# Two transformer blocks on one core: relative products shared by a pair of images, loads image by image, steps re-placed

## The chip, the cores and the metric

The kernel runs on one core of one Trainium2 chip. Its engines work from their own instruction queues and meet only through semaphores: TensorE (PE in the profile, with its weight loads as PEld), VectorE (DVE), ScalarE (ACT), GpSimd (POOL) and SyncE (SP, here the only one that issues DMAs). The metric is the device time of one execution in microseconds, as the median of several.

## The reference

The input is x, 8 images of 16x16 tokens with 192 channels, in float32. It goes through two blocks of the same form, each with its own weights, one after the other:

```
xn = layer_norm(x)                             # eps 1e-5 in block 0, 1e-6 in block 1
windows of 14x14 of xn padded to 28x28         # four windows an image, three of them mostly padding
q, k, v = xn @ qkv_w + qkv_b                   # 12 heads of 16 channels
attn = q*0.25 @ k.T                            # within a window
attn += rel_h[..., :, None] + rel_w[..., None, :]
#   rel_h = einsum("bhwc,hkc->bhwk", q, rel_pos_h[coords]), rel_w alike, along the other axis
out = softmax(attn) @ v
x = x + out @ proj_w + proj_b
x = x + gelu(layer_norm(x) @ fc1_w + fc1_b) @ fc2_w + fc2_b    # 192 -> 768 -> 192, exact gelu
```

Everything is held in float32. Several products are made of high and low parts of a rounded type (F32R), so that they come near float32.

## The kernel before, in words

**Tiling.** An image is 256 tokens, two tiles of 128. X stays in SBUF for all 8 images and both blocks, so there are 16 passes "n" (image n % 8 of block L = n // 8); `par` is n % 2 and chooses one of two buffers. The windows need no padding in memory: a mask row in the stacks keeps tokens of other windows apart, and small steps named pad_* add what the padded keys give to a softmax.

**A pass.** Its steps, in order:

- front: stats1, root1, hat1 normalise; PE transposes (`norm1`, L837, L839); ACT and DVE split the result in high and low parts (L521, L522, L677, L678); the q, k and v products (L831) go one after the other through the one PSUM bank FB, each evacuated by DVE.
- relative products (`front`, L903 to L919): for each of the two axes (w = 0, 1) 14 matmuls, one stationary matrix `rel_heads` (96x84) for each row or column i of the window. Rows 14 and 15 of the image use the matrices of rows 0 and 1, so for i = 0, 1 the moving operand is two rows (64 columns), else one (32 columns). A float32 matmul is two records in the trace. ACT evacuates w = 0 (L555), DVE w = 1 (L715); `rel_tok` (L920) brings what the pads need to token order.
- stacks: ACT, POOL split q, k and rel in high and low parts; SP copies them by DMA (L308, L329) into q_stack and k_stack, together with constant rows for the positions and the mask; one buffer of each for even and one for odd passes, in two groups of 6 heads.
- by_query (L971): scores with queries on partitions, for the row maxima alone (DVE, L768). top and neg_top; SP puts the negated maxima into the stack.
- by_key (L940): scores again with keys on partitions, ACT exponentiates (L530); times_v (L957) multiplies by v_ones, v with a column of ones.
- back: to_tokens (L1053), att, proj (L1040), x_att, stats2, root2, hat2, norm2 (L837 once more), low2, fc1 (L976), gelu (L595), fc2 (L1073), x_mlp.

**Order.** Each engine's program is unrolled by `run` from a table of its own (PE_AT, ACT_AT, DVE_AT, POOL_AT, SP_AT). A table gives each step a tick; step s of pass n is issued at tick 48 n + AT[s], and an engine issues its steps in the order of ticks. Ticks are an order and no times, and they are not comparable from one engine to another. In this way TensorE mixes by_query of pass n, the front of pass n+1, by_key of n-1 and the back of n-2.

**Start.** SP loads image 0, constants and block 0's qkv weights, copies the constant rows into both stacks by DMA (L289), loads the 7 other images at once (L293), then the proj and fc2 weights of both blocks (L294 to L301) on one semaphore `s_w`, then fc1's weights. POOL rounds the constant rows first (L389).

Of the kernel before, what the change touches and what calls it, by code (L numbers as in the profile page):

```python
# [5 lines left out]
F32 = mybir.dt.float32  # L6
F32R = mybir.dt.float32r
ALU = mybir.AluOpType
# [3 lines left out]
P = 128  # L12
# [3 lines left out]
HEADS = 12  # L16
# [11 lines left out]
NV = 3  # L28
# [10 lines left out]
ZEROED = 7 + 2 * NV  # L39
# [3 lines left out]
W_LOADS = 16 * 2 * 5  # L43
# [20 lines left out]
SP_AT = dict(qk0=-10, rel0=2, stack1=37, neg_top=66, wqkv=7, w1=-19, out=213)  # L64
# [5 lines left out]
def build(nc, x, layers, const, out):  # L70
# [3 lines left out]
    with ExitStack() as ctx:  # L74
# [43 lines left out]
        xhat = [sb(f"xhat{i}", [P, TILES, D]) for i in range(2)]  # L118
        xn_hi = [sb(f"xn_hi{i}", [P, 2, TOK], F32R) for i in range(2)]
        rows_rounded = xn_hi[1]  # L120
        xn_lo = [sb(f"xn_lo{i}", [P, TOK], F32R) for i in range(2)]
        q_t = sb("q_t", [GF, 2, TOK])
        k_t = sb("k_t", [GF, 2, TOK])
        q_grid = sb("q_grid", [GF, 2, TOK])
# [4 lines left out]
        rel_t = sb("rel_t", [GR, 2, 2, TOK])  # L129
# [25 lines left out]
        for L in range(2):  # L155
            rel.append(att[0:GF, L, 0:2 * (2 * WS - 1)].rearrange("p (w o) -> p w o", w=2))
# [990 lines left out]
```

## Time and profile before

| | us |
|---|---|
| median of 3 runs | 670.36 (660.64 to 671.58) |
| profiled execution, own time | 666.7 |
| its span, first to last instruction | 664.8 |
| PE busy / PEld busy | 558.1 (84%) / 502.5 (76%) |
| DVE / ACT / POOL busy | 361.0 (54%) / 305.5 (46%) / 236.1 (36%) |
| relative products, L917 | 87.7 busy, 896 records |
| by_query, L971 / row maxima, L768 | 84.8 / 130.7 |
| by_key, L940 / exps, L530 | 89.7 / 103.5 |
| fc2, L1073 | 70.9 |

Matmuls are pipelined, so busy times of neighbours overlap and a group's mean is longer than its pace. PEclk is the clock that TensorE was granted, as a share of its 2.4 GHz; it has two levels, 1.0 and 0.5. A wait names who released the waiting instruction last. The page's slices show PE idle in the third and fourth fortieth of the span and busy at 0.8 to 0.9 from then on.

### The profile page before, as it was taken

How to read it: one execution, taken by the hardware profiler on the slowest of the kernel's cores; microseconds unless marked ns; L12 is line 12 of the kernel's file. 1: busy time of each engine (PE TensorE's matmuls, PEld its weight loads, DVE VectorE, ACT ScalarE, POOL GpSimd, SP SyncE). 2: the span in 40 equal slices, each digit the busy share in tenths (PEclk: the TensorE clock that was granted, in tenths of full speed). 3: DMA queues.
4: the chain of work that ended last, by engine and by line, in shares of the span. 5: the costliest groups of instructions: out<-in, count | busy, mean ns of one | idle time of the engine just before them, and what ended most of it. 6: DMA issues, size and time to landing. Idle time of an engine off the chain costs nothing.

```text
span 664.8 us, 12602 instructions
## 1 busy us (share of the span) xinstructions
PE 558.1 (84%) x4440; PEld 502.5 (76%) x4440; DVE 361.0 (54%) x914; ACT 305.5 (46%) x614; POOL 236.1 (36%) x424
## 2 busy tenths in 40 slices
PE   5700778989898989899998989898989998978766
PEld 4700667779797979798897978797979887967646
DVE  3210265685848484856448575758584767473221
ACT  1100113347463736464344737474745574746522
POOL 2001354253625343441515252354444263430100
PEclk9999977599989898997689988999897999999777
DMA  4416523322222222224112222222231323220000
GB/s 99 107 47 172 107 52 70 85 68 69 52 54 58 58 59 58 59 58 101 42 37 45 61 55 58 59 57 61 57 72 43 86 53 76 57 71 27 1 12 13
DMA packets 45674, 41.10 MB, mean 62 GB/s; under 512 B 6268, under 2 KB 44588, under 8 KB 45612
## 3 DMA queue, kind: packets, MB, share of 16 engines
q1 hardware_dynamic: 45612, 40.29, 25.9%
q8 instruction: 36, 0.59, 0.4%
q14 instruction: 26, 0.21, 0.1%
HBM read 6.80 MB, written 1.57 MB: 13 GB/s over the span
## 4 chain that ended last, share of the span: by engine, by line
PE 55%; issue 13%; DVE 9%; SPq 9%; POOL 8%; ACT 3%; DMA 3%; POOLq 0%; DVEq 0%; ACTq 0%
PE front L917 11%; PE back L831 10%; PE back L1073 9%; PE by_key L940 5%; PE by_query L971 5%; PE front L831 4%; DVE xhat L671 3%; SPq L297 3%; PE times_v L957 2%; POOL norm_rstd L394 2%; SPq L293 2%; POOL pad_e L423 2%; SPq L289 2%; PE back L1053 1%; DVE att L750 1%
## 5 line engine op out<-in xcount | busy, mean ns | idle before, releaser
L768 DVE TENSOR_REDUCE row_max<-by_query 128x2 f32<-128x512 f32 x192 | 130.7, 682 | 48.9 <-PE by_query L971 47.7
L530 ACT ACTIVATE probs<-by_key 128x452 f32<-128x452 f32 x192 | 103.5, 543 | 84.9 <-PE by_key L940 84.3
L940 PE MATMUL by_key<-q_stack,k_stack 110*128 110x196 f32 (+1 forms) x384 | 89.7, 331 | 2.2 <-ACT probs L530 1.9
L971 PE MATMUL by_query<-k_stack,q_stack 108*128 108x256 f32 x384 | 84.8, 314 | 8.0 <-DMA q_stack<-rel_lo 7.7
L917 PEld LDWEIGHTS front<-q_grid,rel_heads 96*84 96x84 f32 x896 | 86.9, 181 | 3.8 <-ACT rel_t L556 1.9
L917 PE MATMUL front<-q_grid,rel_heads 96*84 96x32 f32 (+1 forms) x896 | 87.7, 265 | 2.2 <-ACT rel_t L556 1.4
L940 PEld LDWEIGHTS by_key<-q_stack,k_stack 110*128 110x128 f32 x384 | 63.9, 210 | 14.7 <-issue 7.3
L971 PEld LDWEIGHTS by_query<-k_stack,q_stack 108*128 108x128 f32 x384 | 65.5, 213 | 10.0 <-DMA q_stack<-rel_lo 9.5
L1073 PE MATMUL back<-w,hid 128*128 128x192 f32 x384 | 70.9, 337 | 0.4 <-ACT hid L595 0.3
L1073 PEld LDWEIGHTS back<-w,hid 128*128 128x128 f32 x384 | 65.0, 198 | 1.2 <-ACT hid L595 0.8
L831 PE MATMUL back<-xn_hi,w_hi 128*128 128x256 f32 x192 | 61.3, 328 | 2.7 <-DVE xn_hi L678 2.7
L831 PE MATMUL back<-xn_hi,w_lo 128*128 128x256 f32 x192 | 60.3, 323 | 0.0
L394 POOL TENSOR_TENSOR norm_rstd<-norm_var,minus_half 128x2 f32<-128x2 f32 x32 | 30.0, 939 | 75.4 <-DVE norm_var L663 74.1
L671 DVE TENSOR_TENSOR xhat<-xhat,norm_rstd 128x384 f32<-128x384 f32 x32 | 32.0, 1001 | 42.9 <-POOL norm_rstd L394 42.9
L715 DVE COPY rel_t<-front 84x448 f32<-84x448 f32 x16 | 9.9, 621 | 82.0 <-PE front L917 82.0
L448 POOL TENSOR_TENSOR pad_w<-pad_w,pad_prod 128x36 f32<-128x36 f32 x16 | 4.2, 263 | 138.5 <-ACT pad_w L570 138.5
L831 PEld LDWEIGHTS back<-xn_hi,w_hi 128*128 128x128 f32 x192 | 45.7, 238 | 3.6 <-DVE xn_hi L678 3.6
L957 PE MATMUL times_v<-probs,v_ones 128*32 128x256 f32 (+1 forms) x768 | 48.2, 370 | 0.0
L831 PEld LDWEIGHTS back<-xn_hi,w_lo 128*128 128x128 f32 x192 | 45.2, 236 | 0.0
L488 POOL CAST rel_hi<-rel_t 84x512 fp32r<-84x512 f32 x32 | 19.5, 609 | 71.9 <-DVE rel_t L716 59.0
L595 ACT ACTIVATE hid<-back,b_real 128x256 f32<-128x256 f32 x96 | 38.8, 473 | 10.6 <-PE back L831 10.4
L490 POOL TENSOR_TENSOR rel_lo<-rel_t,rel_hi 84x512 fp32r<-84x512 f32 x32 | 40.8, 1276 | 2.6
(142 smaller groups left out, 1102.7 us busy)
## 6 DMA issues: line engine op xcount, KB each, us to landing
q_stack<-q_hi SPq DMA_DIRECT2D x64, 96.0 KB
k_stack<-k_hi SPq DMA_DIRECT2D x64, 96.0 KB
q_stack<-rel_hi SPq DMA_DIRECT2D x64, 84.0 KB
q_stack<-rel_lo SPq DMA_DIRECT2D x64, 84.0 KB
q_stack<-q_lo SPq DMA_DIRECT2D x32, 96.0 KB
k_stack<-k_lo SPq DMA_DIRECT2D x32, 96.0 KB
out<-X SPq DMA_DIRECT2D x8, 192.0 KB, 2.2
k_stack<-xn_hi SPq DMA_DIRECT2D x2, 744.0 KB
```

Source lines behind the costliest of these rows:

```text
L394: pool.tensor_tensor(norm_rstd[i][:, :], norm_var[i][:, :], minus_half[:, :], ALU.pow).then_inc(n_rstd[i], 1)
L490: pool.tensor_tensor(rel_lo[par][:, w, :, :], rel_t[:, w, :, :], rel_hi[par][:, w, :, :].bitcast(F32), ALU.subtract).then_inc(s_rlo, 1)
L530: act.activation(probs[h % NP][:, :], KB[h % 2][:, 0:KEYS], ACT.Exp).then_inc(s_ex, 1)
L595: act.activation(hid[:, m, :], fc1_psum(m), ACT.Gelu, bias=b1_real[L][:, m:m + 1]).then_inc(s_ge, 1)
L671: dve.tensor_tensor(xhat[i][:, :, :], xhat[i][:, :, :], norm_rstd[i][:, :].unsqueeze(2).broadcast_to([P, TILES, D]), ALU.mult).then_inc(n_ ...
L768: dve.tensor_reduce(row_max[:, h, :], QB[h % 2][:, :].rearrange("p (a t) -> p a t", a=TILES), AX, ALU.max).then_inc(s_smax, 1)
L831: last = pe.matmul(psum, lhs, rhs, start=(i == 0), stop=(i == len(chunks) - 1))
L917: last = pe.matmul(dst[:, :, at, :], rel_heads[L][:, w, WS - 1 - i:2 * WS - 1 - i, :] .rearrange("p k h -> p (k h)"), grid[:, :, at, :], s ...
L940: last = pe.matmul(KB[h % 2][:, lo:hi], k_stack[par][0:ROWS, h, c * P:(c + 1) * P], q_stack[par][0:ROWS, h, 0:hi - lo], start=True, stop=True)
L957: last = pe.matmul(VB[i * VW:(i + 1) * VW, 0:hi - lo], v_ones[n % NV][:, c, h, :], probs[h % NP][:, lo:hi], start=(c == 1), stop=(c == 0))
L971: last = pe.matmul(QB[h % 2][:, a * TOK:(a + 1) * TOK], q_stack[par][0:R_MAX, h, a * P:(a + 1) * P], k_stack[par][0:R_MAX, h, :], start=Tr ...
L1073: last = pe.matmul(BB[0][:, a * D:(a + 1) * D], hid[:, m, a * P:(a + 1) * P], w2[L][:, m, :], start=(m == 0), stop=(m == MC - 1))
```

## The change

1. Relative products are made for a pair of images (n even, n+1). q_grid and rel_t hold both. Each axis is two blocks ("halves") of 8 matmuls; one matmul takes one row (or column) of both images, 64 columns, with one stationary matrix. The steps rel0 and rel1 become `rel` with four places in PE_AT; ACT evacuates two blocks, DVE two. q_t and k_t are double-buffered.
2. The 7 other images are loaded one by one, each with its semaphore. proj_b, fc2_b and the back weights have semaphores of their own by block, and are loaded at `late`. fc1's weights of block 0 come ahead of the first stack loads. The stack constants are written by ACT straight into the stacks (`stack_constants`), not rounded by POOL and copied by DMA. The fc1 bias product goes from pass 1 to pass 2 of a block.
3. Memory: v_ones has 17 columns a head for 32 and 5 buffers for 3; the rest of VB is zeroed once by a DVE memset. pad_e lies in rel_tok, and xhat of norm2 in att, with a wait for each (`s_psum` in rel_tok, `n_tr[1]` in att).
4. All places in the five tables are new. Many steps of the front have a place for even and one for odd passes. SP takes neg_top(n) ahead of stack1(n+1), and all eight stores behind everything else. The three gelu steps stand behind the 12 exps.

The diff, cut:

```diff
-NV = 3
+NV = 5
-ZEROED = 7 + 2 * NV
+ZEROED = 7 + NV
-W_LOADS = 16 * 2 * 5
+W_LOADS = 16 * 3
...
-PE_AT = dict(bias0=-42, bias1=-51, bias2=-48, norm1=-47, q=-41, k=-35, v=-30, rel0=-21, rel1=-15, rel_tok=-11,
-             by_query=(5, 6, 10, 14, 18, 22, 25, 29, 31, 34, 39, 42), neg_top=52,
-             by_key=(56, 60, 62, 65, 72, 76, 77, 81, 83, 87, 92, 96), times_v=(74, 87, 104), to_tokens=106, att=110,
-             proj=114, norm2=123, fc1=(127, 128, 132), fc2=(140, 148))
-ACT_AT = dict(weights1=-45, weights2=40, norm1=-46, q_hi=-35, q_grid=-36, k_hi=-27, rel0=-14, rel_tok=-1, pad_e=26, pad_w=63,
-              att=116, neg_top=51, probs=(62, 64, 68, 74, 76, 78, 82, 86, 90, 95, 99, 103), norm2=124,
-              gelu=(132, 135, 137))
-DVE_AT = dict(stats1=-58, hat1=-52, low1=-47, weights1=-45, weights2=47, bias0=-43, bias1=-50, bias2=-49, setup=-31, q=-42, k=-32, v=-23,
-              rel1=-17, pad_max=15, pad_sum=27, pad_top=34,
-              row_max=(5, 9, 13, 15, 19, 25, 27, 28, 32, 37, 40, 43), top=45, times_v=(78, 88, 105), att=108,
-              x_att=116, stats2=120, hat2=120, low2=123, x_mlp=149)
-POOL_AT = dict(norm_b=-45, root1=-46, proj_bias=-32, pad_shift=23, pad_join=30, pad_arg=59, pad_mul=59, pad_sum=66,
-               pad_out=78, fc2_bias=128, root2=121, q_lo=-21, k_lo=-22, rel0=-6, rel1=-4)
-SP_AT = dict(qk0=-10, rel0=2, stack1=37, neg_top=66, wqkv=7, w1=-19, out=213)
+PE_AT = dict(bias0=-64, bias1=-70, bias2=-74, norm1=(-68, -75), q=(-63, -68), k=(-52, -65), v=(-48, -61),
+             rel=(-5, -2, 0, 7), rel_tok=(17, 7), by_query=(41, 42, 48, 50, 51, 59, 60, 67, 70, 71, 74, 75),
+             neg_top=78, by_key=(84, 86, 91, 92, 94, 95, 101, 102, 103, 106, 109, 111), times_v=(101, 115, 123),
+             to_tokens=131, att=141, proj=144, norm2=157, fc1=(165, 169, 173), fc2=(173, 175))
+ACT_AT = dict(constants=(-83, 0), weights1=-80, weights2=98, norm1=(-54, -58), q_hi=-7, q_grid=(2, -46), k_hi=0,
+              rel=(7, 15), rel_tok=(31, 31), pad_e=58, pad_w=110, att=154, neg_top=94,
+              probs=(99, 101, 103, 105, 109, 111, 114, 118, 119, 121, 128, 129), norm2=169, gelu=(178, 183, 186))
+DVE_AT = dict(stats1=(-111, -114), hat1=(-92, -101), low1=(-67, -73), weights1=-84, weights2=82, bias0=-66,
+              bias1=-71, bias2=-87, setup=-46, q=(-59, -68), k=(-53, -68), v=(-52, -61), rel=(-4, 3), pad_max=28,
+              pad_sum=43, pad_top=58, row_max=(37, 42, 43, 44, 45, 53, 55, 56, 64, 67, 73, 74), top=75,
+              times_v=(100, 110, 126), att=133, x_att=139, stats2=141, hat2=141, low2=150, x_mlp=176)
+POOL_AT = dict(norm_b=-110, root1=(-158, -157), proj_bias=(-118, 19), pad_shift=-22, pad_join=-4, pad_arg=29,
+               pad_mul=42, pad_sum=42, pad_out=71, fc2_bias=104, root2=102, q_lo=-59, k_lo=-59, rel0=(-37, -91),
+               rel1=(-35, -75))
+SP_AT = dict(x=-878, late=-274, qk0=-350, rel0=-347, stack1=-328, neg_top=-283, wqkv=-254, w1=-356, out=1733)
...
-            for par in range(2):
-                sp.wait_ge(s_rounded, 1)
-                for stack, lo, hi, c in ((q_stack, R_MASK, R_MAX, 1), (k_stack, R_RHI, ROWS, 0)):
-                    sp.dma_start(stack[par][lo:hi, :, :].bitcast(F32),
-                                 rows_rounded[lo:hi, c:c + 1, :].bitcast(F32).broadcast_to([hi - lo, HEADS, TOK])
-                                 ).then_inc(s_stack0[par], 16)
-                if par == 0:
-                    sp.dma_start(X[:, TILES:, :], x_t[:, TILES:, :]).then_inc(s_x, 16)
-            for L in range(2):
+
+            def load_late(L):
                 p = layers[L]
-                for tile, name in ((pb[L], "proj_b"), (b2[L], "fc2_b")):
-                    sp.dma_start(tile[:, :], p[name].unsqueeze(0).broadcast_to([P, D])).then_inc(s_w, 16)
+                if L == 1:
+                    sp.dma_start(pb[1][:, :], p["proj_b"].unsqueeze(0).broadcast_to([P, D])).then_inc(s_pb[1], 16)
+                sp.dma_start(b2[L][:, :], p["fc2_b"].unsqueeze(0).broadcast_to([P, D])).then_inc(s_b2[L], 16)
                 sp.wait_ge(s_wz, L + 1)
-                sp.dma_start(wp[L][:, 0, :], p["proj_w"][0:P, :]).then_inc(s_w, 16)
-                sp.dma_start(wp[L][0:LO, 1, :], p["proj_w"][P:D, :]).then_inc(s_w, 16)
-                sp.dma_start(w2[L][:, :, :], p["fc2_w"].rearrange("(m f) n -> f m n", f=P)).then_inc(s_w, 16)
-            sp.wait_ge(s_wxl, 1)
-            sp.wait_ge(s_wxh, 2)
-            sp.wait_ge(s_bx, 1)
-            load_w1(0)
+                sp.dma_start(wp[L][:, 0, :], p["proj_w"][0:P, :]).then_inc(s_w[L], 16)
+                sp.dma_start(wp[L][0:LO, 1, :], p["proj_w"][P:D, :]).then_inc(s_w[L], 16)
+                sp.dma_start(w2[L][:, :, :], p["fc2_w"].rearrange("(m f) n -> f m n", f=P)).then_inc(s_w[L], 16)
+
+            def setup(n, L, par, t):
+                if t == SP_AT["x"] and 1 <= n < IMAGES:
+                    sp.dma_start(x_slot(0, n), x_t[:, n * TILES:(n + 1) * TILES, :]).then_inc(s_x[n], 16)
+                if t == SP_AT["late"] and n in (0, 2):
+                    load_late(n // 2)
...
+                    if n < 2:
+                        sp.wait_ge(s_stack0, 2 * (n + 1))
...
+                    src = rel_t[:, w, 2 * par:2 * par + 2, :]
+                    pool.wait_ge(s_relo, 4 * (n // 2) + 2 * w + 2)
+                    for g in range(2):
+                        if n >= 2:
+                            pool.wait_ge(*stack_loaded(n - 2, g))
+                    pool.tensor_copy(rel_hi[par][:, w, :, :], src).then_inc(s_rhi[par], 1)
+                    pool.wait_ge(s_rhi[par], done)
+                    pool.tensor_tensor(rel_lo[par][:, w, :, :], src, rel_hi[par][:, w, :, :].bitcast(F32),
+                                       ALU.subtract).then_inc(s_rlo[par], 1)
...
+            def stack_constants(par):
+                act.wait_ge(s_rows, 32)
+                for stack, rows in ((k_stack, key_rows), (q_stack, query_rows)):
+                    act.activation(stack[par][:, :, :], rows.unsqueeze(1).broadcast_to([P, HEADS, TOK]),
+                                   ACT.Copy).then_inc(s_stack0, 1)
+
             def weights(n, L, par, t):
+                if t in ACT_AT["constants"] and n == 0:
+                    stack_constants(ACT_AT["constants"].index(t))
...
+                if t in ACT_AT["rel"] and par == 0:
+                    half = ACT_AT["rel"].index(t)
+                    act.wait_ge(s_rel, 2 * n + half + 1)
+                    if n > 0:
+                        act.wait_ge(s_rt, n)
+                        for i in range(2):
+                            act.wait_ge(s_rlo[i], n)
+                    rows = slice(half * 8, half * 8 + 8)
+                    out, src = rel_t[:, 0, :, :], FB[0:GR, :].rearrange("p (m r c) -> p m r c", m=4, c=SIDE)
+                    act.activation(tall(out)[:, :, rows, :], src[:, :, :, 0:WS], ACT.Copy)
+                    act.activation(edge(out)[:, :, rows, :], src[:, :, :, WS:SIDE], ACT.Copy).then_inc(s_relo, 1)
...
+                if t in DVE_AT["rel"] and par == 0:
+                    half = DVE_AT["rel"].index(t)
+                    dve.wait_ge(s_rel, 2 * n + 3 + half)
+                    if n > 0:
+                        dve.wait_ge(s_rt, n)
+                        for i in range(2):
+                            dve.wait_ge(s_rlo[i], n)
+                    out, src = rel_t[:, 1, :, :], FB[0:GR, :].rearrange("p (m c r) -> p m r c", m=4, r=SIDE)
+                    if half == 0:
+                        last = dve.tensor_copy(tall(out)[:, :, :, 0:8], src)
+                    else:
+                        dve.tensor_copy(tall(out)[:, :, :, 8:WS], src[:, :, :, 0:WS - 8])
+                        last = dve.tensor_copy(edge(out), src[:, :, :, WS - 8:8])
+                    last.then_inc(s_relo, 1)
...
-                    for i in range(WS):
-                        at = slice(i, i + WS + 1, WS) if i < EDGE else slice(i, i + 1)
-                        last = pe.matmul(dst[:, :, at, :], rel_heads[L][:, w, WS - 1 - i:2 * WS - 1 - i, :]
-                                         .rearrange("p k h -> p (k h)"), grid[:, :, at, :], start=True, stop=True)
+                        pe.wait_ge(s_relo, 2 * n + 2 * w + half)
+                    grid = q_grid[:, :, :].rearrange("p m (r c) -> p m r c" if w == 0 else "p m (r c) -> p m c r", c=SIDE)
+                    dst = FB[0:GR, :].rearrange("p (m r c) -> p m r c", m=4, c=SIDE)
+                    for j in range(8):
+                        i = (half * 8 + j) % WS
+                        last = pe.matmul(dst[:, :, j, :], rel_heads[L][:, w, WS - 1 - i:2 * WS - 1 - i, :]
+                                         .rearrange("p k h -> p (k h)"), grid[:, :, half * 8 + j, :], start=True, stop=True)
                     last.then_inc(s_rel, 1)
...
```

Other lines of the diff give the new semaphores, choose the `[par]` place of a step, and index q_t and k_t by par.

## Rows read from the trace of the kernel before

**Rows 1.** The page's first line.

```profile
span 664.8 us, 12602 instructions
```

**Rows 2.** Windows: start:end, length, busy time (instructions) by engine, TensorE clock, DMA share, GB/s.

```profile
519.30:582.00 62.70, 58.68 (x541) 53.12 (x541) 41.58 (x103) 37.16 (x74) 28.32 (x49) 1.00 0.28 68
...
582.00:664.80 82.80, 61.09 (x417) 51.25 (x415) 29.93 (x79) 35.52 (x64) 11.61 (x25) 0.83 0.09 25
...
129.20:519.30 390.10, 363.71 (x3038) 331.95 (x3037) 247.50 (x626) 211.55 (x427) 160.62 (x275) 0.90 0.26 59
...
77.60:129.20 51.60, 43.92 (x304) 39.01 (x305) 30.02 (x73) 14.34 (x35) 21.97 (x41) 0.73 0.33 71
```

**Rows 3.** Chain of waits at the start: start us, us, what.

```profile
5.06 2.76 DMA hid<-c_query_rows
...
10.15 14.94 SPq L293
...
34.31 15.12 SPq L297
...
74.45 3.15 DMA q_stack<-rel_lo
```

**Rows 4.** Waits of the run: who for whom, us in total, times, longest.

```profile
POOL X L399 <- DMA w<-in_fc_w: 55.2, 1, 55.2
...
PE front L844 <- DMA weights_in<-in_fc_w: 30.8, 1, 30.8
```

**Rows 5.** Waits from 129.2 to 582 us.

```profile
PE back L837 <- DVE xhat L671: 20.9, 13, 1.8
```

**Rows 6.** Timelines (start, length, engine, what, idle time before) and a window: a norm2 stop.

```profile
212.12 0.41 PE L837 MATMUL back<-ident,xhat 128*128 128x128 f32 x2 [1.76 <-DVE xhat L671]
...
212.00:219.00 7.00, 6.88 (x49) 6.89 (x50) 3.88 (x9) 3.39 (x7) 5.64 (x13) 0.63 0.13 33
...
5.45 0.56 DVE L671 TENSOR_TENSOR xhat<-xhat,norm_rstd 128x384 f32<-128x384 f32 x1 [0.60 <-POOL norm_rstd L394]
...
279.73 1.61 DVE L671 TENSOR_TENSOR xhat<-xhat,norm_rstd 128x384 f32<-128x384 f32 x1 [0.59 <-POOL norm_rstd L394]
```

**Rows 7.** Relative products: timelines of four 64-column records each, one block on the chain.

```profile
287.39 0.61 PE L917 MATMUL front<-q_grid,rel_heads 96*84 96x64 f32 x4
...
361.80 0.45 PE L917 MATMUL front<-q_grid,rel_heads 96*84 96x64 f32 x4
...
287.56 2.21 PE front L917 x28
```

**Rows 8.** Timeline of the start, image 0's front and the fc1 bias product.

```profile
6.15 0.66 PE L837 MATMUL front<-ident,xhat 128*128 128x128 f32 x2 [6.15 <-DVE xhat L671]
...
7.82 1.43 ACT L500 ACTIVATE wqkv_hi<-weights_in,columns 128x576 fp32r<-128x576 f32 x2
...
8.39 0.42 DVE L678 TENSOR_TENSOR xn_hi<-front,xn_hi 64x256 fp32r<-64x256 f32 x1
...
14.02 0.53 PE L831 MATMUL front<-xn_hi,wqkv_hi 128*96 128x256 f32 x1
...
24.00 4.13 PE L917 MATMUL front<-q_grid,rel_heads 96*84 96x64 f32 x28 [0.65 <-DVE v_ones L705]
...
28.87 4.13 PE L917 MATMUL front<-q_grid,rel_heads 96*84 96x64 f32 x28 [0.74 <-ACT rel_t L556]
...
66.15 0.58 PE L844 MATMUL front<-columns,weights_in 128*128 128x1 f32 x2 [30.76 <-DMA weights_in<-in_fc_w]
...
73.14 0.66 PE L837 MATMUL front<-ident,xhat 128*128 128x128 f32 x2 [0.77 <-DVE b_real L623]
```

**Rows 9.** Timeline of SyncE's queue: two kinds of stack loads.

```profile
69.84 0.60 SPq L308 DMA_DIRECT2D k_stack<-k_hi  x1
...
71.76 1.80 SPq L329 DMA_DIRECT2D q_stack<-rel_hi  x2
```

**Rows 10.** Groups by line: name, shapes, count, busy us, mean ns, idle before.

```profile
L595 ACT ACT_TABLE_LOAD x31 | 39.8, 1283 | 0.5
```

More of the change, by code:

```diff
@@ L117, in build @@
         norm_rstd = [sb(f"norm_rstd{i}", [P, TILES]) for i in range(2)]
-        xhat = [sb(f"xhat{i}", [P, TILES, D]) for i in range(2)]
         xn_hi = [sb(f"xn_hi{i}", [P, 2, TOK], F32R) for i in range(2)]
-        rows_rounded = xn_hi[1]
         xn_lo = [sb(f"xn_lo{i}", [P, TOK], F32R) for i in range(2)]
-        q_t = sb("q_t", [GF, 2, TOK])
-        k_t = sb("k_t", [GF, 2, TOK])
-        q_grid = sb("q_grid", [GF, 2, TOK])
+        q_t = [sb(f"q_t{i}", [GF, 2, TOK]) for i in range(2)]
+        k_t = [sb(f"k_t{i}", [GF, 2, TOK]) for i in range(2)]
+        q_grid = sb("q_grid", [GF, 4, TOK])
         q_hi = [sb(f"q_hi{i}", [GF, 2, TOK], F32R) for i in range(2)]
@@ L135, in build @@
         k_stack = [sb(f"k_stack{i}", [P, HEADS, TOK], F32R) for i in range(2)]
-        v_ones = [sb(f"v_ones{i}", [P, TILES, HEADS, VW]) for i in range(NV)]
-        pad_e = sb("pad_e", [P, 2 * HEADS, WS])
+        v_ones = [sb(f"v_ones{i}", [P, TILES, HEADS, HD + 1]) for i in range(NV)]
+        pad_e = rel_tok[:, 0:2 * HEADS * WS].rearrange("p (h k) -> p h k", k=WS)
         seg_max = [sb(f"seg_max{i}", [P, 2, HEADS]) for i in range(2)]
@@ L154, in build @@
         att = sb("att", [P, TILES, 2 * P])
+        xhat = [sb("xhat", [P, TILES, D]), att[:, :, 0:D]]
         for L in range(2):
@@ L210, in build @@
         s_rt, s_rto = sem("rel_transposed"), sem("rel_tok_ready")
-        s_rhi, s_rlo = sem("rel_hi"), sem("rel_lo")
+        s_rhi, s_rlo = ([sem(f"{x}{i}") for i in range(2)] for x in ("rel_hi", "rel_lo"))
         s_v = sem("v_ready")
@@ L517, in norm_hi @@
                 act.wait_ge(s_vp if i == 0 else s_f1, n if i == 0 else MC * n)
-                if i == 1 and n == 0:
-                    for par in range(2):
-                        act.wait_ge(s_stack0[par], 32)
                 act.activation(xn_hi[i][:, 0, :], bank[:, 0:TOK], ACT.Copy)
@@ L582, in norms @@
             def norms(n, L, par, t):
-                if t == ACT_AT["norm1"]:
+                if t == ACT_AT["norm1"][par]:
                     norm_hi(0, n, FB)
@@ L896, in front @@
                                           slice(at + g * GF, at + (g + 1) * GF))
-                    last.then_inc(s_qp if t == PE_AT["q"] else s_kp, 1)
-                if t == PE_AT["v"]:
+                    last.then_inc(s_qp if t == PE_AT["q"][par] else s_kp, 1)
+                if t == PE_AT["v"][par]:
                     pe.wait_ge(s_kto, n + 1)
@@ L902, in front, with rel_products @@
                     last.then_inc(s_vp, 1)
-                if t in (PE_AT["rel0"], PE_AT["rel1"]):
-                    w = (PE_AT["rel0"], PE_AT["rel1"]).index(t)
-                    if w == 0:
-                        pe.wait_ge(s_v, n + 1)
-                        pe.wait_ge(s_qg, n + 1)
+            def rel_products(n, L, par, t):
+                if t in PE_AT["rel"] and par == 0:
+                    w, half = divmod(PE_AT["rel"].index(t), 2)
+                    if w + half == 0:
+                        pe.wait_ge(s_v, n + 2)
+                        pe.wait_ge(s_qg, n + 2)
@@ L922, in front, with rel_tokens @@
+                    last.then_inc(s_rel, 1)
+            def rel_tokens(n, L, par, t):
+                if t == PE_AT["rel_tok"][par]:
+                    if par == 0:
+                        pe.wait_ge(s_relo, 2 * n + 4)
+                    elif n + 1 < 2 * IMAGES:
+                        pe.wait_ge(s_v, n + 2)
+                    else:
+                        pe.wait_ge(s_rto, n)
                     for w in range(2):
@@ L956, in times_v @@
                             h = g * QUAD + i
[L957 removed]
+                            last = pe.matmul(VB[i * VW:i * VW + HD + 1, 0:hi - lo], v_ones[n % NV][:, c, h, :],
                                              probs[h % NP][:, lo:hi], start=(c == 1), stop=(c == 0))
@@ L1075, in back @@
                     last.then_inc(s_f2, 1)
-            run(PE_AT, biases, stacks, middle, front, back, times_v, scores_by_key, to_tokens)
+            run(PE_AT, biases, stacks, middle, front, rel_products, rel_tokens, back, times_v, scores_by_key, to_tokens)
 def kernel(**inputs):
```

180 lines of the change are left out of this document (76 added, 104 removed).

## The prediction

> **What bounds the kernel now.** I read the page, the chain, the waits, then single stretches. The span is 664.8 us [rows 1]. Four stretches, cut at the first by_query product of images 0, 2, 13 and 15, show what each is worth [rows 2]. (a) Up to 77.65 us nothing of the scores runs. The reader is to see in the chain that SyncE's queue holds it [rows 3]: the 1344 KB load of X occupies it for 14.94 us, and after a copy of constants the first bias broadcast 15.12. GpSimd then waits 55.2 us for the last back weight, because `s_w` counts both layers, and TensorE 30.8 us for fc1's weights [rows 4]. (b) Images 0 to 2: 51.6 us for two periods. (c) 129.2 to 582.0: 13 periods. TensorE is busy 363.7 of 390.1 us, then 58.7 of 62.7; it is the bound. A period is 390.1/11 = 35.5 us at clock 0.90, but 62.7/2 = 31.4 us where the clock is 1.00. (d) The last 82.8 us, busy 61.1, clock 0.83.
>
> In (c) there is one repeated stop: the norm2 transposes wait 20.9 us in 13 times for xhat [rows 5]. In the stop at 212.12 it lasts 1.76 us, and the seven microseconds from 212 have a clock of 0.63 [rows 6]. In that chain VectorE's multiplication takes 1.61 us; at the start of the kernel, with GpSimd idle, the same took 0.56 [rows 6]. In steady state GpSimd works on k_lo beside it.
>
> **Relative products.** Before: per image 14 stationaries for each of two axes, two records each, 56 records. After: per pair 4 blocks of 8 matmuls, 64 records of 64 columns instead of 112 of mostly 32; over the run 512 for 896. A block of 28 takes 2.21 us on the chain at clock 1.00 [rows 7], 0.075 us a record allowing for its wider ones. Four 64-column records of the column axis, which reads with a stride of 16 elements, cover 0.61 us where four of the row axis cover 0.45 [rows 7]: 0.16 more, of which I give 0.05 to the last one's own length, so about 0.11 us a record against 0.075. Before, a pair is 56 x 0.075 + 48 x 0.075 + 8 x 0.11 = 8.7 us; after, 32 x 0.075 + 32 x 0.11 = 5.9. That is 2.8 a pair, 1.4 an image, all on the bound. Bounds: 0.075 for all (3.9 a pair) and 0.61/4 = 0.15 for the strided (1.5 a pair): 9 us less and 10 more over the run.
>
> The Trainium skill, "TensorE: Matmul & The Clock Gate", Back-to-back issue gap, has every product of 1 to 64 columns cost the same, which would be the first of these bounds: 31 us saved in all where my rows say 22. The strided row is what speaks against it here.
>
> Between the four blocks one bank is evacuated: 0.74 us at the start (28.13 to 28.87) [rows 8]. In the steady order two by_key heads, and sometimes the att transposes, stand between rel.0 and rel.1, only two heads between rel.1 and rel.2, and much between rel.2 and rel.3. I charge 1 us a pair, 6.5 over 13 periods. The by_key and by_query heads now go in twos against two banks; 0.1 us of wait a period is 1.5. Together **+8**; bounds 0 and +20 (four uncovered evacuations of 0.74 in each of 6.5 pairs).
>
> **Start.** X goes as 192 KB loads, fc1's as soon as qkv's buffer is free, proj and fc2 weights after image 1's stacks. The pieces of X still need the queue, but image 1 needs only the first of them, and nothing else is wanted before some 36 us; cover gone, it costs up to 14.94 us. The stack constants come from ScalarE. Two qkv weight activations of 576 columns take 1.43 us [rows 8], so 3072 columns at about 0.9 ns each are 2.9 us, two per parity 5.8 (upper bound 7.6 at 1.24 ns). The rows' transfer took 2.76 [rows 3], is now second in the queue, lands near 4.5; the constants end at 10.3, weights at 11.8, norm_hi and the low part at 13.5. Before, q starts at 14.02, after the bias product [rows 8]; I take 14.5. q, k, v are 10 us (14.02 to 24.00): 24.5. Image 1 has to go through FB too before the first rel block: 2.7 us from transposes (6.15) to low part (8.81), plus 10: 37.2. ScalarE's second pair of constants, 5.8 us, fits beside that. Four blocks at the start's pace of 4.13 x 16/28 = 2.36, plus 0.74 each: 49.6. rel_tok, eight small records at that pace, and one evacuation: about 2.2 (an estimate), 51.8. The fc1 bias product, moved to image 2, is ahead of the first by_query: 7.0 us to the next transposes (66.15 to 73.14) [rows 8], then norm1(2) 2.7 and q(2) 2.3 (two thirds of a third of the 10 us above): **64**. The stack of image 0 lands before: GpSimd's two parts of the last axis (2 us, an estimate), SyncE's four issues at 0.9, landing 3.15 [rows 3, 9] make 58.4. So 77.65 becomes 64; bounds 58 (bias product at full clock) and 78 (no gain).
>
> **Norm2.** Between proj and norm2 the order now has four by_query and four or five by_key heads, one times_v group and rel_tok or rel.3: 42 records or more at 58.7/541 = 0.11 us [rows 2], 4.5 us. The chain from proj to xhat lost 1.76 us to a shorter cover with hat2 at 1.61; fc2_bias, which waits for hat2, and not k_lo now follows root2, so a microsecond of the chain goes as well. The stop goes: **-20.9** in (c). What is late next is hat2 itself in VectorE's queue, behind row maxima, covered by one more microsecond only. Bounds 0 and -25.
>
> **Clock.** At 0.90 over 390.1 us, 39.0 us are lost. Behind the stop of [rows 6] the clock fell, and the stretch without a fall is the one in which I take the stops to be shorter. Not every fall need have that cause, so I take two thirds back: **-26**, bounds 0 and -39. The same skill page, in the table of why this matters, warns only of long idle gaps between bursts, so by it stops this short would not lower the clock and this term would be nothing: that is rival A. That 519.3 to 582.0 stayed at 1.00 is for my view [rows 2].
>
> **Other edits at no cost.** Gelus stand in one group after the exps: table loads fall from 31 for gelu (and as many back) to 16, 1.28 us each [rows 10]. ScalarE is busy 37.2 of 62.7 us [rows 2], so it counts only in (d), where gelu and exp alternate on the chain: -3 there. New waits: att waits for norm2's transposes of the image before (xhat shares it), two microseconds or more ahead in the order; rel_tok waits for pad_sum, since pad_e shares it, with 36 of 48 ticks between; rel_hi and rel_lo wait for the stack of n-2, loaded a period earlier. q_t and k_t doubled only remove waits. v_ones at 17 columns, NV 5, a memset of VB: nothing. The eight stores are issued after the last neg_top; the first six are of finished images and go beside some 60 us of TensorE work. w1 and qkv reloads wait on SyncE for scaled halves as before.
>
> **Sum.** (a) 64; (b) 51.6 - 2.8 = 48.8; (c) 452.8 - 18.2 - 20.9 - 26 + 8 = 395.7; (d) 80: 588.5 us of span. The profiled execution took 666.7 for 664.8, so 590.4. It lay 3.7 us under the median of the three runs (670.36); put back, **594 us**.
>
> **Rivals.**
> A. The stops move rather than go, and the clock stays (for: another wait lies one microsecond behind; that every fall has its stop isn't shown; against: the 31.4 us periods). Then (c) is 452.8 - 18.2 + 8 = 442.6 and the median 641. Chance 0.15.
> B. The start gives nothing: two fronts, constants and the bias product take until 78 us. For: three tasks were put in front; against: 30 us of queueing in [rows 3] are gone. 608. Chance 0.08.
> C. Slower. SyncE takes neg_top(n) before the second half of stack n+1 and all of n+2. Place: by_query's seventh head of image n+1. After neg_top(n), six issues at 0.60 and four at 0.9 plus 3.15 of landing are 10.4 us [rows 3, 9]; TensorE's order up to that head holds about half of a period, 15 us. From 4.6 us of extra delay (the qk rows held by by_key of n-1, or k_lo late behind GpSimd's rel parts) each further microsecond costs 15. At 6.5 beyond it 98 are lost, more than the 76 gained: about 692. The queue's waits before, and by_query not among the long waits in (c), speak against. Chance 0.03.
> D. Strided products at 0.15 us or evacuations uncovered: the rel part saves almost nothing, 594 + 20 = 614. Chance 0.08.
> My forecast, 0.66: 570 to 615.
>
> **Range.** Down: all of the clock (-13), no new hand-offs (-8), bias product fast (-3) give 570. Up: D, B, and a part of A up to 638, where the clock returns by little. What is left out is most of A's upper half and C, about a tenth, and somewhat less below. A measurement of this kernel tells about 2% (13 us) from no change. Faster by more than that: A, B, D and the forecast, 0.94 with a margin for the unforeseen; within, 0.03; slower 0.03.
>
> **What would show it.** L917 with 512 records, the four-record test 0.45 and 0.61; first by_query near 64; no wait of back L837 over 1 us; table loads halved; periods near 30 us with clock over 0.95. By_query waiting for q_stack's transfer is C, L837 or another back wait of 1.5 us with the clock at 0.90 is A. It is wrong if periods stay at 33 us or more.

## The result and the profile after

The changed kernel takes 545.72 us (median of 4 runs, 545.31 to 546.63) where the kernel before took 668.19 beside it (660.64 to 671.58): ratio 0.82, 95% interval 0.8124 to 0.8275. Ratios are of fast executions alone; where the kernel before stands beside a run below, its time is the median of those of its executions that lie within 1.5% of the fastest. The forecast was 594, the range 570 to 638. The direction was right; the gain was 1.6 times the forecast one, 122 us instead of 76.

The page after: span, TensorE's busy tenths and the clock's.

```profile
span 543.9 us, 11882 instructions
...
PE   2777878889999999999999999999999999999947
...
PEclk9999998989999999999979999999999999999988
```

The profiled execution took 545.7 us for this span. TensorE is busy for 90% or more of each slice from the tenth to the thirty-eighth, and the clock's row has hardly a dent. Cut at the same places, first by_query of images 0, 2 and 15 (columns as in [rows 2]):

```profile
0.00:65.70 65.70, 43.15 (x198) 37.76 (x199) 19.64 (x58) 20.67 (x28) 19.19 (x41) 1.00 0.36 84
65.70:109.60 43.90, 36.55 (x284) 29.12 (x283) 32.02 (x76) 15.40 (x39) 23.76 (x43) 0.96 0.42 92
109.60:476.30 366.70, 362.23 (x3191) 328.57 (x3190) 275.27 (x701) 209.47 (x463) 177.88 (x316) 0.99 0.33 75
476.30:543.90 67.60, 53.11 (x389) 44.39 (x388) 27.27 (x75) 27.45 (x58) 10.91 (x24) 0.92 0.13 35
```

Stretch (c) as one window of the kernel before:

```profile
129.20:582.00 452.80, 422.38 (x3577) 385.07 (x3576) 289.07 (x729) 248.71 (x501) 188.94 (x324) 0.92 0.26 60
```

So (a) went from 77.6 to 65.7, (b) from 51.6 to 43.9, (c) from 452.8 to 366.7, (d) from 82.8 to 67.6. In (c) the norm2 stops of [rows 5] are gone. The longest wait of TensorE left there (columns as in [rows 4]); the only other one is 1.5 us in all:

```profile
PE front L844 <- DVE q_t L695: 2.4, 2, 1.6
```

VectorE's second multiplication, the 1.61 us of [rows 6], is short in steady state now (timeline). Relative records are 512, as forecast, and table loads for gelu 15, where the forecast had 16 (groups by line as in [rows 10]):

```profile
297.58 0.56 DVE L677 TENSOR_TENSOR att<-att,norm_rstd 128x384 f32<-128x384 f32 x1
```

```profile
L931 PE MATMUL front<-q_grid,rel_heads 96*84 96x64 f32 x512 | 56.4, 273 | 4.0 <-ACT rel_t L562 2.5
```

### The profile page after: what moved, and what is told of

Read it like the earlier page. It is cut to its first block, busy times and chain, and to the rows that moved or that the text cites. A ratio compares the mean times of both kernels' runs of the same rounds, so it can differ in the third digit from the quotient of the medians.

```text
span 543.9 us, 11882 instructions
## 1 busy us (share of the span) xinstructions
PE 495.0 (91%) x4056; PEld 439.8 (81%) x4056; DVE 354.2 (65%) x907; ACT 273.0 (50%) x586; POOL 231.7 (43%) x422
## 4 chain that ended last, share of the span: by engine, by line
PE 81%; issue 9%; DVE 6%; ACT 1%; DMA 1%; POOL 1%; SPq 1%; DVEq 0%; ACTq 0%; POOLq 0%
PE back L844 14%; PE front L844 12%; PE back L1094 10%; PE front L931 10%; PE by_key L961 9%; PE by_query L990 8%; PE times_v L978 7%; DVE row_max L782 1%; PE front L858 1%; PE front L949 1%; PE front L857 1%; PE front L850 1%; PE back L1074 1%; PE front L946 1%; PE back L850 1%
## 5 line engine op out<-in xcount | busy, mean ns | idle before, releaser
L961 PE MATMUL by_key<-q_stack,k_stack 110*128 110x196 f32 (+1 forms) x384 | 73.5, 308 | 1.5 <-ACT probs L532 1.2
L990 PE MATMUL by_query<-k_stack,q_stack 108*128 108x256 f32 x384 | 69.4, 295 | 1.4 <-DVE row_max L782 1.0
L414 POOL TENSOR_TENSOR rel_tok<-rel_tok,seg_max 128x48 f32<-128x48 f32 (+1 forms) x32 | 14.6, 479 | 115.4 <-DVE seg_max L739 115.4
L961 PEld LDWEIGHTS by_key<-q_stack,k_stack 110*128 110x128 f32 x384 | 53.6, 193 | 11.2 <-issue 5.5
L931 PE MATMUL front<-q_grid,rel_heads 96*84 96x64 f32 x512 | 56.4, 273 | 4.0 <-ACT rel_t L562 2.5
L931 PEld LDWEIGHTS front<-q_grid,rel_heads 96*84 96x84 f32 x512 | 53.0, 173 | 5.7 <-ACT rel_t L562 3.3
L844 PE MATMUL front<-xn_hi,wqkv_hi 128*96 128x256 f32 x128 | 40.7, 327 | 9.8 <-DVE q_t L695 4.9
L978 PE MATMUL times_v<-probs,v_ones 128*17 128x256 f32 (+1 forms) x768 | 47.5, 366 | 0.0
L844 PE MATMUL front<-xn_hi,wqkv_lo 128*96 128x256 f32 x128 | 38.0, 306 | 0.0
L844 PEld LDWEIGHTS front<-xn_hi,wqkv_hi 128*96 128x96 f32 x128 | 23.4, 183 | 15.4 <-DVE xn_hi L684 8.2
```

Source lines behind the costliest of these rows:

```text
L414: last = pool.tensor_tensor(pad_e[:, :, lo:hi], pad_e[:, :, lo:hi], m.broadcast_to([P, 2 * HEADS, hi - lo]), ALU.subtract)
L844: last = pe.matmul(psum, lhs, rhs, start=(i == 0), stop=(i == len(chunks) - 1))
L931: last = pe.matmul(dst[:, :, j, :], rel_heads[L][:, w, WS - 1 - i:2 * WS - 1 - i, :] .rearrange("p k h -> p (k h)"), grid[:, :, half * 8 + ...
L961: last = pe.matmul(KB[h % 2][:, lo:hi], k_stack[par][0:ROWS, h, c * P:(c + 1) * P], q_stack[par][0:ROWS, h, 0:hi - lo], start=True, stop=True)
L978: last = pe.matmul(VB[i * VW:i * VW + HD + 1, 0:hi - lo], v_ones[n % NV][:, c, h, :], probs[h % NP][:, lo:hi], start=(c == 1), stop=(c == 0))
L990: last = pe.matmul(QB[h % 2][:, a * TOK:(a + 1) * TOK], q_stack[par][0:R_MAX, h, a * P:(a + 1) * P], k_stack[par][0:R_MAX, h, :], start=Tr ...
```

## Experiments

Theory: a short stop of TensorE ahead of norm2 costs its own length and, behind it, clock; the clock gave back more than the forecast's 26 us. Rival: stop and clock are separate, and the surplus comes from fewer records or fewer table loads. Clock loss below is (1 - mean clock) x span of the profiled run; it is 65 us in the kernel before (0.902 x 664.8) and 12 in the changed one (0.978 x 543.9). It leaves out the start: the trace's record of the clock begins with the first change of level, at 80.6 us in the kernel before and at 68.1 in the changed one, and the rows' 1.00 ahead of that is no reading. The products show the level instead: 256 columns start 0.21 us apart until just before 68 us in the changed kernel and 0.12 apart behind it, and the kernel before goes from one distance to the other at 80.6 us.

### Edits of the kernel before

These four ran beside a kernel before of 656.1 us (four runs, 652.27 to 660.28; all seven reach to 678.25). Its mean clock in these four was 0.914 to 0.927, a clock loss of about 51 us.

**Stop filled.** Ahead of the norm2 transposes:

```
+ for _ in range(7):
+     pe.matmul(BB[0][:, 0:P], ident[:, :], ident[:, :], start=True, stop=True)
```

> The kernel before, with 7 throwaway 128x128 products of the identity (1.5 us at clock 1.00) on TensorE between the two waits of the norm2 transposes, so that the stop before them is as long but not idle; BB[0] is free there. Theory (the idle stops lower the clock, and the clock's return was the term of the sum mis-sized): nothing else changes, the clock from 129 to 582 us rises from 0.90 to 0.97 or more and the time falls by 20 to 35 us, to about 640. Rival (the clock falls for another reason, such as what TensorE computes, and what the change gained is the stops themselves): no change, 668 within 4, clock 0.90.

Measured 638.76 us (637.41 to 645.04), ratio 0.9774 (0.9677 to 0.987), 17 us less, a little under the 20 to 35 expected. From 129 to 582 us the clock is 0.98 where it was 0.92, and the clock loss is 31 us in the profiled run, the slowest of the four, and 20 to 26 in the others. TensorE's waits ahead of norm2 fell from 27.4 us to 1.3, but the 224 records of useless work are busy for 31.2 us in their place. So the time came from the clock and not from the stops.

**fc2_bias in front of root2**, so that GpSimd is done sooner for norm2:

```
-               pad_out=78, fc2_bias=128, root2=121, ...
+               pad_out=78, fc2_bias=121, root2=121, ...
```

> The kernel before, one place altered: GpSimd's fc2_bias, which waits for hat2, goes ahead of k_lo and q_lo, so that VectorE's hat2 runs with GpSimd idle. Both theories: hat2 goes from 1.6 to 0.56 us and the norm2 stop from 1.78 to about 0.75 us, 16 us in all. Theory of the clock: the shorter stops cost no clock either, 630 to 640. Rival: 652, clock 0.90.

Measured 626.71 us (625.07 to 628.06), ratio 0.957 (0.951 to 0.9629). VectorE's multiplication took 0.55 us in the mean instead of 1.00, the stops nearly halved, and the clock rose to 0.945, a loss of 34 us:

```profile
PE back L837 <- DVE xhat L671: 14.6, 15, 3.5
```

The stops gave 12.8 us of the 27.4 that all 16 had (16 expected); the time fell by 29, and the clock loss by some 17. A little below the expected window, and far from the rival.

**norm2 one tick later, fc1 two to four**, and **both edits**:

```
-              proj=114, norm2=123, fc1=(127, 128, 132), fc2=(140, 148))
+              proj=114, norm2=124, fc1=(131, 132, 134), fc2=(140, 148))
```

> The kernel before with the norm2 transposes behind the first relative block on TensorE (tick 124 for 123) and the fc1 pairs at 131, 132, 134 for 127, 128, 132. The 1.78 us stop is covered by 2.1 us of products. Theory of the clock: stops (22 us) and most of the clock (25 us) are gained, 620 to 630. Rival: the stops alone, 646. If the stop only moves to fc1: 668.

> The two edits before this together: GpSimd's fc2_bias ahead of k_lo, norm2 and fc1 later on TensorE. One stop can be gained once only: as the better of the two, within 5 us, 620 to 628 by the theory of the clock, 646 by the rival.

Both missed. The later norm2 gave 725.72 us (724.88 to 728.15), ratio 1.109 (1.1003 to 1.1178), clock 0.851; both edits 681.51 (676.2 to 684.61), ratio 1.0399 (1.0298 to 1.05), clock 0.914. The stop had not gone, it had moved to the relative products, where TensorE waits for the evacuation of v, which stands behind hat2 in VectorE's order. In the kernel with norm2 later:

```profile
PE front L917 <- DVE v_ones L705: 25.1, 13, 2.2
```

This is rival A's mechanism, met in another kernel than the changed one. Its stops, most of them of 2.1 us where those of before had 1.8, come with a clock loss of 108 us, about 57 more than beside it, and 12 of the 13 were followed by a fall of the clock within 2.8 us. That fits the theory, but the time rose by 70 us, and with 4 us more of stops ahead of norm2 and the relative products together not all of it is accounted for.

### Edits of the changed kernel

**norm2 earlier**, and **the same with the stop filled**. One number in TensorE's order brings the stop back; the second kernel adds the seven products of above in it.

```
-              to_tokens=131, att=141, proj=144, norm2=157, ...
+              to_tokens=131, att=141, proj=144, norm2=150, ...
```

> The changed kernel with PE's norm2 step at tick 150 instead of 157, which puts the transposes of norm2 ahead of work that covered the way to hat2, so TensorE should stop there again for 1.5 to 2 us per image, 25 to 30 us in 16. Theory (short stops at norm2 lower TensorE's clock, and what follows runs at half of it): the stops' own 25 us and another 15 to 30 of clock, so 585 to 600 us and a mean clock of 0.93 to 0.95. Rival (stop and clock have nothing to do with each other; the gain came from fewer records and fewer table loads): the stops alone, 570 us, clock at 0.98.

> As the kernel with norm2 at tick 150, but while TensorE would stand still for norm2 it does seven throwaway products of the identity (128 columns) into a bank that is written over at once. Its work and its order are otherwise the same. Theory (the idle stop lowers the clock): no clock loss, only the 1.5 to 2 us that the fillers take, so 568 to 575 us, clock 0.98, some 20 us faster than the same kernel without the fillers. Rival (the clock falls for another reason): the same time as without the fillers, or longer.

Measured 626.36 us (625.66 to 629.27) and 580.53 us (580.42 to 582.89), on the same chip. The mean clock is 0.888 in the first and 0.982 in the second. First norm2 earlier: its norm2 stops in the whole run, one of them, and three windows about it; then the stops of the filled kernel.

```profile
PE back L850 <- DVE att L677: 36.7, 16, 3.5
```

```profile
365.58 0.57 PE L850 MATMUL back<-ident,att 128*128 128x128 f32 x2 [2.30 <-DVE att L677]
```

```profile
352.00:365.60 13.60, 11.30 (x113) 10.41 (x111) 10.43 (x30) 5.55 (x14) 8.94 (x19) 1.00 0.44 100
365.60:379.40 13.80, 13.80 (x79) 12.37 (x80) 6.19 (x13) 5.69 (x12) 8.06 (x9) 0.51 0.10 26
379.40:390.00 10.60, 10.60 (x91) 9.85 (x90) 7.64 (x20) 7.10 (x13) 5.54 (x7) 1.00 0.12 32
```

```profile
PE back L850 <- DVE att L677: 9.4, 16, 0.9
```

The reader is to see: TensorE stands still for 2.30 us; then it is busy 13.80 of 13.80 us, at half clock, and does 79 records where the stretch behind, which is 3.2 us shorter, holds 91. The last image aside, 12 of 15 stops were followed by such a stretch, of 3 to 21 us, that began within 2.0 us of the stop's end; three were not. (In the kernel before it is 7 of the ten stops of 1.75 to 1.78 us, within 2.6 us, and none of the two of 1.2 us between 519 and 582, where the clock stayed at 1.00; one of 0.7 us had a fall behind it too.) Filled, the stops shrink to 9.4 us and the clock stays. The pair differs in nothing else, and the fillers' 28.5 us with the 9.4 of waits left take the room of the 36.7. So 45.8 us are the clock's, and the 34.8 above the changed kernel are the stops' own. I had put the clock's share at 15 to 30, norm2 earlier at 600 at most and the filled kernel at 575 at most: all too low. This pair settles that such stops cost clock, and what it costs. By clock loss it differs by 69.9 - 10.4 = 59.5, so that measure overstates the price by about a third. Not all work doubles at the slow level: a strided block of 16 relative records takes 2.41 us in that stretch (from 366.80) and 1.94 at full speed.

**Relative products twice as many**, one image each:

```
-  last = pe.matmul(dst[:, :, j, :], ..., grid[:, :, half * 8 + j, :], ...)
+  for m in (0, 2):
+      last = pe.matmul(dst[:, m:m + 2, j, :], ..., grid[:, m:m + 2, half * 8 + j, :], ...)
```

> The changed kernel with each relative product of 64 columns (two images) split into two of 32 columns (one image each), that is 1024 records for 512; everything else stays. By the prediction's prices (75 ns a record on the row axis and 111 ns on the strided one, for 32-column records 75 ns each, part of the strided ones 111) a pair of images takes 9.6 to 11 us where it took 5.9, +29 to +40 us over the run, if TensorE is the bound and the time goes by the number of records: 575 to 586 us. Rival (64 columns cost twice what 32 cost, so the time goes by columns): no change, 546 us.

Measured 590.53 us (589.39 to 592.27), 44.8 more, 5 above the expected window. First by_query of images 2 and 15 come at 126.4 and 519.8, so (c) is 393.4 us, 26.7 more than in the changed kernel for 6.5 pairs, 4.1 a pair. About 3.5 of it are the products: a block of 32 records takes 2.53 us on either axis, where one of 16 takes 1.35 to 1.40 on the row axis and 1.94 on the strided one. On the row axis 64 columns cost no more than 32; on the strided one they cost half as much again. So the rival (by columns) fell.

The rest is clock, most of it lost without a stop. Two windows, ahead of a fall in this kernel and behind it; the fall comes at 230.96 us, behind a block of 32 records of 32 columns:

```profile
224.00:231.00 7.00, 7.00 (x91) 6.34 (x90) 4.45 (x12) 2.30 (x4) 4.79 (x12) 1.00 0.41 85
231.00:234.40 3.40, 3.40 (x19) 3.33 (x19) 2.64 (x6) 1.63 (x4) 3.32 (x4) 0.50 0.00 0
```

TensorE is busy 7.00 of 7.00 us, and the clock falls for 3.4 us. The same happened at 480.1. The changed kernel has no fall at these places of its order. In (b) this kernel has a fall of 13.7 us, in such a block, with no stop over 0.2 us in the 4 us before it: the clock of (b) is 0.87 where the changed kernel has 0.96, and (b) 51.8 us for 43.9. Another 8.9 us lie ahead of image 0, where all runs at the slower pace. So the rival of the first filled kernel (the clock falls for another reason, such as what TensorE computes) is true beside the theory, for a part of the falls.

**gelu.0 between two exps**, `gelu=(176, 183, 186)` for `(178, 183, 186)`:

> The changed kernel with the first gelu group placed between two exps instead of after the last, so that ScalarE loads its table some 30 times more (30 x 1.28 = 38 us of ScalarE). Theory (ScalarE stands beside TensorE and is not on the path, except at the end): +3 to +8 us, 549 to 554. Rival (table loads were a good part of the gain): up to +38 us, 584.

Measured 567.82 us (567.75 to 568.67), 22 more: neither. ScalarE has 60 table loads, as many as before but two, and here they reach TensorE:

```profile
PE times_v L978 <- ACT probs L532: 14.1, 13, 1.9
```

14.1 us of stops and 7.3 more clock loss (19.3 for 12.0, clock 0.966) come to about the 22. In the kernel before no wait of TensorE for probs ahead of times_v is among the twenty longest, though it loaded as many tables. So the grouping keeps the new order free of a stop; that it would gain anything in the order of before is not shown, and nothing in its waits says so.

### The start and the end, and a better version

The four ran on one chip; the kernel before took 663.9 us there (six runs, 659.98 to 666.99; all eleven reach to 677.1).

> The changed kernel itself once more, beside the three that follow, so that a few microseconds can be read on the same chip. By every theory 545 to 547 us.

Measured 546.38 us (544.93 to 550.13).

**Fillers in the start**, in images 0 and 1, and **the fc1 bias product spread** between relative blocks:

```
+ def warm(n, k):
+     if n < 2:
+         for _ in range(k):
+             pe.matmul(BB[0][:, 0:P], ident[:, :], ident[:, :], start=True, stop=True)
+ ... warm(n, 6) ahead of q, warm(n, 4) of k and v, warm(n, 3) of each relative block, ...
```

```
+ if n == 0 and w + half > 0:
+     fc1_bias_pair(w * 2 + half - 1)
```

> The changed kernel with throwaway products of the identity in the waits of the start: eight ahead of the first bias product, and for images 0 and 1 six ahead of q, four ahead of k and of v, three ahead of each relative block and of rel_tok. In the changed kernel a 256-column product takes 0.415 us in the first 66 us, the 1.2 GHz pace, though the page grants 1.00 there. Theory (TensorE runs at the lower of its two levels as long as its work is broken by stops of about 1 us): with the gaps filled the pace doubles on the way and the first by_query comes 8 to 20 us sooner, 526 to 538 us in all. Rival (the start is slow for another reason, or the fillers cost what they give): no gain, up to 6 us more, 546 to 552.

> The changed kernel with the fc1 bias product of layer 0 (6.2 us in one piece at 54.1 to 60.3 us) done in three pairs of columns between the relative blocks of image 0, into another bank, where TensorE waits 0.74 us for each evacuation. Theory of the sum (the start is a chain that TensorE sets): about 3 x 0.7 us hidden and the rest of the 6.2 still there, and the last block no later: -2 to -5 us, 541 to 544. Rival (the first by_query waits for something else): 546.

> The changed kernel with the two edits of a_warm and a_bias_spread and with throwaway products also in the last image's stops (7 ahead of att, 2 ahead of proj, 14 ahead of norm2, 6 ahead of fc1). Theory (idle stops lower the clock at the end too: 0.77 and 0.79 over the last 24 us): 3 to 6 us at the end, and 10 to 25 at the start: 517 to 532. Rival: nothing at either end, 541 to 550.

The start with fillers: 536.72 us (535.27 to 540.18), ratio to before 0.8094 (0.8046 to 0.8142) where the changed kernel has 0.8246 (0.8188 to 0.8304): 9.7 us faster, as expected. Products of 256 columns in the start, first in the changed kernel, then with fillers (start, length):

```profile
19.67 0.41 PE L844 MATMUL front<-xn_hi,wqkv_lo 128*96 128x256 f32 x1
19.89 0.41 PE L844 MATMUL front<-xn_lo,wqkv_hi 128*96 128x256 f32 x1
```

```profile
19.29 0.28 PE L844 MATMUL front<-xn_hi,wqkv_lo 128*96 128x256 f32 x1
19.41 0.28 PE L844 MATMUL front<-xn_lo,wqkv_hi 128*96 128x256 f32 x1
```

They start 0.21 to 0.22 us apart in one and 0.12 in the other. The Trainium skill, "TensorE: Matmul & The Clock Gate", "Wait — 56ns, not 53.3ns?", has columns by 1.2 GHz for the slow level and columns by 2.4 GHz plus 2.5 ns for the fast one; worked out from that, an estimate, 256 columns are 213 and 109 ns. The rows agree, to 0.01 us. The first by_query came 10.2 us sooner (65.7 to 55.5), but the next two images took 48.4 us for 43.9, at a clock of 0.79:

```profile
55.50:103.90 48.40, 41.48 (x284) 33.09 (x284) 32.05 (x76) 15.43 (x39) 23.68 (x43) 0.79 0.40 86
```

The spread bias product: 547.56 us (544.16 to 552.06), no change that can be told from the 546.38, so the 2 to 5 us expected did not come. Its first by_query came at 62.5 instead of 65.7, as the sum of the start has it, but (b) took 45.8 for 43.9 at a clock of 0.89.

All together, with fillers in the last image too: 536.58 us (535.59 to 538.73), ratio 0.8089 (0.8046 to 0.8132), not to be told from the fillers in the start alone, and above the 517 to 532 expected. In the last stretch the clock loss went, though, and 3.6 us with it: from 469.8 to 533.8 us the clock is 1.00, and (d) takes 64.0 us instead of 67.6.

## Why the prediction was wrong

**Start.** Right. The constants took 2.77 and 2.75 us (2.9 forecast), the first relative block began at 38.65 us (37.2), blocks followed at 3.25 us (3.1), first by_query 65.7 (64). The queueing of [rows 3] was the bound, and no part of X was missed.

**Relative products.** Right in price: 512 records, and two blocks of 16 at the fast level took 1.41 us on the row axis and 1.98 on the strided one (timeline of the kernel with fillers in the start), 36 ns a record between them, as the 0.075 and 0.11 us a record have it. Splitting them again cost about 3.5 us a pair in products. The bounds were off by a little: they changed the price of a record after and left the 8.7 of before, which goes with it, so they are 3.6 and 1.8 us a pair, not 3.9 and 1.5, and the first saves 29 us in all, not 31.

**Norm2.** Right: the 20.9 us went and did not come back elsewhere. The 1.61 us multiplication is 0.56, and GpSimd does nothing beside it: its next work waits 0.67 us for just that multiplication:

```profile
298.22 1.01 POOL L394 TENSOR_TENSOR X<-X,b 128x384 f32<-128x384 f32 x1 [0.67 <-DVE att L677]
```

With norm2 seven ticks earlier the stops were back though the multiplication was as short there (mean of 16: 0.56 us), so the cover in TensorE's order is needed. What the shorter multiplication alone is worth was measured in the kernel before only: with fc2_bias in front of root2, 12.8 us of stops and 29 us of time.

**Clock: the step that failed.** The term was 26 us, two thirds of the 39.0 lost in 129.2 to 519.3, and nothing for (b) and (d). By the windows' clocks (c) lost 36.2 us before (0.92) and 3.7 after (0.99): 32.5 back. And (b) lost 13.9 (0.73 of 51.6 us) and now 1.8, and (d) 14.1 (0.83 of 82.8) and now 5.4. Both clocks stood in [rows 2] and were quoted, and no return was put on either. In all the clock loss fell by 53.3 us where the term had 26. At the rate of the filled pair (45.8 us of time for 59.5 of loss) the 53.3 are about 41, an estimate: 25 in (c), close to the term, 9 in (b) and 7 in (d). So the mechanism held in (c), and what was mis-sized is the term as a whole, by 15 us at that rate and 27 by the clocks.

The cause that I gave covers (c) only. The two long falls of (b) in the kernel before, 17.1 us each, began at 90.9 and 118.2 in blocks of 28 relative records, with no stop over 0.2 and 0.5 us in the 4 us before them. In the changed kernel (b) has one fall, of 3.4 us; with its products split to 32 columns again it has the one of 13.7. That points to the shape of the products and not to a wait, but no run isolates it for (b). For (d), fillers in the last image's stops brought the clock to 1.00.

The rule that I weighed against this term, that only long idle gaps matter, was no help: 12 of 15 stops of 2.1 to 2.3 us had a fall behind them. The same page of the Trainium skill ("TensorE: Matmul & The Clock Gate", "A second HAM failure mode: psum-queue depth-cycling") also has a kernel in which "the PE micro-idles between MM groups frequently enough that HAM oscillates"; the traces here agree in so far as short stops recur and the clock goes to and fro, with another cause of the stops.

**Sum.** A second error was plain bookkeeping. The forecast of (a) took in the front of image 1, a third of image 2's and the relative products of a pair, and (c) was still charged for 13 of each. The q, k and v products of the fronts in (c) fell from 390 to 350 records, that is 40 at 0.12 us, 4.8 us, and by 728 relative records (13 images) that became 384 (12) it is 21.2 us cheaper instead of 18.2. Together 4.8 + 3.0.

**Hand-offs.** +8 was wrong: in (c) TensorE was idle 30.4 us before and 4.5 after, 25.9 less where the stops alone were 20.9. Ahead of the 384 relative records of (c) TensorE was idle 0.0 us: the heads between two blocks cover the evacuation.

What makes the 48.4 us between 594.1 and 545.7, with the clock by the windows' mean clocks. At the rate of the filled pair the first row is 12.3 us smaller, and the rest of (c) 7.5, of (b) 2.8 and of (d) 2.0 us larger:

| part of the miss | us |
|---|---|
| clock: (c) 6.5, (b) 12.1, (d) 8.7 | 27.3 |
| work counted in (a) and in (c) | 7.8 |
| hand-offs that didn't come | 8.0 |
| (c): other idle time 5.0, rest 1.7 | 6.7 |
| (d), without the clock | 3.7 |
| 3.7 added for the median of before, which the median after doesn't have over its profile | 3.8 |
| (a) later than forecast | -1.7 |
| (b), without the clock: 220 records beside the relative ones for 192 | -7.2 |
| sum | 48.4 |

**Rivals.** A's mechanism exists (norm2 later in the kernel before), its condition wasn't met. B, C and D did not occur: among the twenty longest waits of TensorE is none of by_query for q_stack's transfers, and the start gave what it should. The range failed downwards: 570 was built from all of the clock in (c) and no hand-offs, and held no clock for (b) and (d) and nothing for the work counted twice.

**Falls without a stop.** The clock fell once in the middle of the changed kernel, for 6.8 us at 272.9, and TensorE stood still for none of the time before it:

```profile
266.00:272.90 6.90, 6.90 (x65) 6.11 (x63) 3.40 (x7) 4.64 (x10) 6.66 (x8) 1.00 0.05 14
272.90:279.70 6.80, 6.80 (x40) 5.67 (x40) 3.50 (x9) 1.35 (x3) 0.91 (x2) 0.50 0.15 41
```

What runs from 270.07 to 274.20 is the fc1 bias product, 24 records of one column. In the kernel before two of the falls in (c), at 299.1 and 343.5, came within 1 us of the bias products of qkv and of fc1, with at most 0.03 us of idle time in the 4 us before; so did one in each filled kernel (289.8 and 332.1). So a stop is enough for a fall, most times, but it is not needed.

**Open.** Why three of the 15 stops had no fall behind them (all three were of 2.14 to 2.16 us; the six of 2.30 all had one), and how much of the clock's return is owed to wider relative products.

## What to carry to other kernels

A short stop that recurs on the engine that bounds costs more than its length: here 45.8 us of clock for 36.7 us of idle time. Price it from every window in which the clock is low, not from the one where the stop was found, and look at what the engine did before each fall, since some came without a stop. Test it by filling the stop with useless products, which adds work and shows the clock's share at once. When steps move across a cut between stretches, count the records on both sides, or the same work stands in two terms.

## What the runs showed of the hardware

- A stop of 2.1 to 2.3 us in a TensorE that is otherwise busy was followed by 3 to 21 us at 1.2 GHz in 12 of 15 cases (norm2 earlier); with the stops filled the lower level held for 21 us of the run instead of 141.
- The clock also fell while TensorE had been busy without a stop: in a run of 24 one-column records (changed kernel, 272.9 us, for 6.8 us) and behind a block of 32 records of 32 columns (relative products split, 231.0 us, for 3.4 us).
- The trace records the granted clock from its first change on. Until 68.1 us the changed kernel's products run at the pace of 1.2 GHz (0.21 us for 256 columns) though the rows show 1.00. With fillers in the gaps of about 1 us the record begins at 11.1 us, the products are 0.12 us apart at 19.3 us, and the low stretches show (0.88 over the first 55.5 us).
- Relative products of 64 columns: a block of 16 takes 1.35 to 1.40 us on the row axis and 1.94 on the axis with a stride of 16 elements. Of 32 columns, a block of 32 takes 2.53 us on either.
- With fillers in the start the clock fell at 45.2 us, in the fc1 bias product, 0.8 us behind a stop of 0.79 us; pairs of its one-column records stood 0.29 us apart before the fall and 0.52 after it.
